# Attention groups 8 to 47: probabilities divided before they are split, and multiplied with V in column tiles

## What is computed

```python
# x, ctx: (16, 128, 1024); 32 heads in 8 groups; head width 32; K and V have 8 heads
query, key, value = layernorm(x) @ w_q.T, ctx @ w_k.T, ctx @ w_v.T
scores = einsum('bghnd,bgsd->bghns', query, key) / 32 ** 0.5
scores = where(mask, scores, finfo.min)
out    = einsum('bghns,bgsd->bghnd', softmax(scores), value)
x = x + out @ w_out.T
x1, x2 = split(layernorm(x) @ w12.T + b12)
x = x + (silu(x1) * x2) @ w3.T + b3
```

## Time and profile before

| | |
|---|---|
| median of 3 runs | 1041.44 us (1040.89 to 1043.1) |
| the profiled execution, first to last instruction | 1040.4 us |
| PE busy | 1017.7 us, 98% |
| DVE busy | 661.6 us, 64% |
| ACT busy | 447.3 us, 43% |
| POOL busy | 498.6 us, 48% |
| chain that ended last: PE's share | 87% |

### The profile page before, as it was taken

The page is one execution under the profiler, slowest core; times in us unless marked ns, Lnnn a source line. Parts: engine busy times, 40 slices in busy tenths (PEclk is TensorE's granted clock), DMA queues, the critical chain, the costliest instruction groups (busy, mean ns, idle before and its releaser), DMA issues.

```text
span 1040.4 us, 21876 instructions
## 1 busy us (share of the span) xinstructions
PE 1017.7 (98%) x8400; PEld 695.6 (67%) x8400; DVE 661.6 (64%) x2080; ACT 447.3 (43%) x983; POOL 498.6 (48%) x476
## 2 busy tenths in 40 slices
PE   7897999999999999999999999999999999999998
PEld 6786868869687696886655544444444888468853
DVE  6789977767787777888646234636864447625431
ACT  6768556557465574664766210123431112202100
POOL 2869923727337273379958596158742301212000
PEclk9999999999999999999999999999999999999999
DMA  9669686998989999789946715494758631974201
GB/s 367 227 160 197 168 216 168 222 247 222 248 211 229 230 245 244 179 236 232 268 94 123 253 71 203 94 345 160 272 200 185 235 112 40 236 230 122 83 31 51
DMA packets 230776, 199.12 MB, mean 191 GB/s; under 512 B 177040, under 2 KB 187280, under 8 KB 225808
## 3 DMA queue, kind: packets, MB, share of 16 engines
q1 hardware_dynamic: 230672, 197.72, 69.0%
HBM read 119.04 MB, written 35.65 MB: 149 GB/s over the span
## 4 chain that ended last, share of the span: by engine, by line
PE 87%; DVE 6%; DMA 1%; ACT 1%; issue 0%; SPq 0%; DVEq 0%
PE bank_dense L1349 52%; PE bank_spare L1349 13%; PE bank_score L1494 6%; PE bank_spare L1494 6%; PE bank_av L1494 3%; PE bank_score L1406 2%; DVE arena_attn L1820 2%; DVE arena_attn L1830 1%; PE bank_av L1424 1%; PE bank_av L1428 1%; PE bank_av L1426 1%; PE bank_dense L1366 1%; DMA k_scratch<-arena_in 1%; PE bank_spare L1358 0%; PE bank_dense L1358 0%
## 5 line engine op out<-in xcount | busy, mean ns | idle before, releaser
L1153 ACT ACTIVATE arena_attn<-arena_attn,arena_in 128x128 f32<-128x128 f32 x512 | 162.7, 391 | 94.6 <-DVE arena_in L1820 93.6
L1349 PE MATMUL bank_dense<-arena_rows,arena_in 128*128 128x256 f16 (+1 forms) x1272 | 175.2, 295 | 1.9 <-POOL arena_in L874 1.0
L936 POOL TENSOR_TENSOR arena_attn<-arena_attn 128x512 f16<-128x512 f32 x89 | 102.6, 1170 | 148.8 <-ACT arena_attn L1160 148.8
L1349 PE MATMUL bank_dense<-arena_attn,arena_rows 128*128 128x512 f16 x768 | 166.4, 379 | 0.0
L1349 PEld LDWEIGHTS bank_dense<-arena_rows,arena_in 128*128 128x128 f16 x1272 | 123.0, 98 | 43.1 <-DVE arena_in L1668 1.6
L1820 DVE CUSTOM_DVE_ANT_0 arena_attn<-bank_score,arena_in 128x128 f32<-128x128 f32 x512 | 143.5, 346 | 0.4 <-PE bank_score L1406 0.4
L1349 PEld LDWEIGHTS bank_dense<-arena_attn,arena_rows 128*128 128x128 f16 x768 | 75.2, 98 | 90.2
L1349 PE MATMUL bank_dense<-arena_out,arena_attn 128*128 128x512 f16 x576 | 127.8, 379 | 0.0
L1349 PEld LDWEIGHTS bank_dense<-arena_out,arena_attn 128*128 128x128 f16 x576 | 55.5, 98 | 63.3
L1349 PE MATMUL bank_spare<-arena_rows,arena_in 128*128 128x256 f16 (+1 forms) x648 | 87.6, 292 | 0.0
L1349 PE MATMUL bank_dense<-arena_out,arena_in 128*128 128x512 f16 x384 | 83.0, 379 | 0.0
(11 more groups left out here) (219 smaller groups left out, 1890.8 us busy)
## 6 DMA issues: line engine op xcount, KB each, us to landing
arena_rows<-x SPq DMA_DIRECT2D x32, 512.0 KB, 6.1
arena_in<-w_scratch SPq DMA_DIRECT2D x64, 256.0 KB, 3.1
arena_attn<-q_scratch SPq DMA_DIRECT2D x48, 256.0 KB, 4.5
arena_rows<-w_t SPq DMA_DIRECT2D x12, 1024.0 KB, 6.2
arena_rows<-ctx_t SPq DMA_DIRECT2D x8, 1024.0 KB, 6.1
q_scratch<-arena_attn SPq DMA_DIRECT2D x16, 512.0 KB, 5.1
x_scratch<-arena_rows SPq DMA_DIRECT2D x16, 512.0 KB, 3.8
arena_out<-x_scratch SPq DMA_DIRECT2D x16, 512.0 KB, 5.9
```

The source lines that it names most:

```text
L936: ins = pool.tensor_tensor(p_split[:, g % 2, u, 1], e[:, g % 2, u], p_split[:, g % 2, u, 0], ALU.subtract)
L1153: ins = act.activation(head, head, ACT.Exp, bias=neg_max[:, g % 2, h:h + 1], scale=-1.0)
L1349: ins = pe.matmul(dst, lhs(a, c), rhs(b, c), start=(c == chunks[0] and n == 0), stop=(c == chunks[-1] and n == 2))
```

## The change

For groups 8 to 47 (`NORMED`) the probabilities are divided by their sum before they are split into fp16 pairs, and the product with V is taken the other way round:

- **ACT** `exps`: each of the 8 exponentials also sums its output into `p_sum` (`accum_out`). `prob_hi(g)` no longer waits for the exponentials but for the division (`s_vnorm`, `s_pnorm`), and stands behind `scale_rows`.
- **DVE** `norm_prob(g, 0)` behind `attn_lo(g-3)` in step g, and `norm_prob(g, 1)` at the head of step g+1, ahead of `divide` and `mask_scores(g+1)`. Each is a reciprocal of 4 sums and a multiply of 512 columns of `e` in place, with the reciprocals broadcast. The reciprocals lie in SBUF for g = 8 and 9 and in `bank_av` (PSUM) from 10 on.
- **POOL** `norm_prob(g)`: where s is 3 or more it does the multiply of sequence 0; DVE then only scales the 4 reciprocals for it. In its order it stands behind `prob_lo(g-1)`.
- **PE** `weigh(g)`: V's 32 columns are the weights and the turned probabilities (128 columns) the moving operand; each of the four heads of a sequence has its own 32 columns of the array (`tile_position=(0, 32 j)`). 24 matmuls as before. The result is already turned; it goes to a bank of the rotation, in `turn_attn`'s place in step g+3, and `turn_attn(g)` and `divide(g)` are gone. The weigh at the end of step g+2 is gone too.
- `attn_hi`, `attn_lo` take the factor 2^-14 out again. Waits that meant "weigh(g) done" now look at `s_dense`; SP's `turn_prob(g)` waits for `weigh(g-2)`, which comes one step later than it did.

```diff
+NORMED = range(8, 48)
+P_SCALE = 2.0 ** 14
+def by_pool(g):
+    return g in NORMED and g % GROUPS >= 3
...
+        def weighed(g):
+            return (s_dense, done("a", g)) if g in NORMED else (s_av, divided_count(g))
...   (SP, turn_prob; PE and ACT wait in the same way)
                 if g >= 2:
-                    sp.wait_ge(s_av, g - 1)
+                    sp.wait_ge(*weighed(g - 2))
...   (POOL)
+            def norm_prob(g):
+                pool.wait_ge(s_vinv, normed_count(g, by_pool))
+                heads = e[:, g % 2, 0].rearrange("p (j n) -> p j n", j=HPG)
+                pool.tensor_tensor(heads, heads, inv.rearrange("p (j o) -> p j o", o=1).broadcast_to([P, HPG, SEQ]),
+                                   ALU.mult).then_inc(s_pnorm, 1)
...
-                    if GROUPS * (t - 1) + s > PLO_ALONE:
-                        prob_lo(GROUPS * (t - 1) + s - 1)
+                    g = GROUPS * (t - 1) + s
+                    if g > PLO_ALONE:
+                        prob_lo(g - 1)
+                    if by_pool(g):
+                        norm_prob(g)
...   (ACT)
-                    ins = act.activation(head, head, ACT.Exp, bias=neg_max[:, g % 2, h:h + 1], scale=-1.0)
+                    if g in NORMED:
+                        ins = act.activation(head, head, ACT.Exp, bias=neg_max[:, g % 2, h:h + 1], scale=-1.0,
+                                             accum_out=p_sum[:, g % 2, u, j:j + 1])
+                    else: ...
...
             def prob_hi(g):
-                act.wait_ge(s_exp, 2 * g + 2)
+                if g in NORMED:
+                    act.wait_ge(s_vnorm, vector_count(g, 1))
+                    if by_pool(g):
+                        act.wait_ge(s_pnorm, normed_count(g, by_pool))
+                else:
+                    act.wait_ge(s_exp, 2 * g + 2)
...   (PE, weigh)
+                if g in NORMED:
+                    dst = begin("a", g)
+                    terms_of_out = ((v_high, 0), (v_low, 0), (v_high, 1))
+                    for u in range(U):
+                        for n, (v, piece) in enumerate(terms_of_out):
+                            for j in range(HPG):
+                                ins = pe.matmul(dst[DH * j:DH * j + DH, SEQ * u:SEQ * u + SEQ],
+                                                v[:, a % 2, u, m, 0:DH], prob_t[:, g % 2, u, piece, j],
+                                                start=n == 0, stop=n == 2, tile_position=(0, DH * j))
+                    ins.then_inc(s_dense, 1)
+                    return
...
-                    if g >= 3:
+                    if g >= 3 and g - 3 in NORMED:
+                        weigh(g - 3)
+                    elif g >= 3:
                         turn_attn(g - 3)
...
-                    if g >= 2:
+                    if g >= 2 and g - 2 not in NORMED:
                         weigh(g - 2)
...   (DVE)
+            def norm_prob(g, u):
+                sums_inv = (inv_first if g < NORMED[2] else inv_bank)[:, g % 2, u]
+                dve.wait_ge(s_exp, 2 * g + u + 1)
+                dve.reciprocal(sums_inv, p_sum[:, g % 2, u]).then_inc(s_rec, 1)
+                dve.wait_ge(s_rec, half_count(g, u))
+                if u == 0 and by_pool(g):
+                    dve.tensor_scalar(inv, sums_inv, P_SCALE, None, ALU.mult).then_inc(s_vinv, 1)
+                    return
+                heads = e[:, g % 2, u].rearrange("p (j n) -> p j n", j=HPG)
+                dve.scalar_tensor_tensor(out=heads, in0=heads, scalar=P_SCALE,
+                                         in1=sums_inv.rearrange("p (j o) -> p j o", o=1).broadcast_to([P, HPG, SEQ]),
+                                         op0=ALU.mult, op1=ALU.mult).then_inc(s_vnorm, 1)
...   (DVE's program)
+                    if g - 1 in NORMED:
+                        norm_prob(g - 1, 1)
                     if g >= 3:
                         divide(g - 3)
                     mask_scores(g)
...
                     if g >= 3:
                         attn_lo(g - 3)
+                    if g in NORMED:
+                        norm_prob(g, 0)
```

More of the change, by code:

```diff
@@ L302, in later_unit, with normed_count, half_count, vector_count @@
     return UNITS * (f - PLAIN) + i
+def by_pool(g):
+    return g in NORMED and g % GROUPS >= 3
+def normed_count(g, kind=lambda n: n in NORMED):
+    return sum(kind(n) for n in range(g + 1))
+def half_count(g, u):
+    return U * normed_count(g - 1) + u + 1
+def vector_count(g, u):
+    return half_count(g, u) - normed_count(g, by_pool)
+def divided_count(g):
+    return g + 1 - normed_count(g)
 def plo_count(g):
@@ L409, in xattn_ffn @@
         kept, with_6, with_5, with_7 = [terms[:, 0], terms[:, 1]], terms[:, 2], terms[:, 3], terms[:, 4]
+        p_sum = part(arena_attn, 59, 1, F32)[:, 0:2 * U * HPG].rearrange("p (r u j) -> p r u j", r=2, u=U)
+        inv = part(arena_attn, 60, 1, F32)[:, 0:HPG]
+        inv_first = part(arena_attn, 61, 1, F32)[:, 0:2 * U * HPG].rearrange("p (r u j) -> p r u j", r=2, u=U)
         k_stack = part(arena_attn, 63, 4).rearrange("p (b g n) -> p b g n", b=2, g=4)
@@ L559, in xattn_ffn @@
         s_av, s_inv, s_avread = sem("av_done"), sem("inv_sum_done"), sem("attn_ready")
+        s_pnorm, s_vnorm = sem("prob_normed_by_pool"), sem("prob_normed_by_vector")
+        s_rec, s_vinv = sem("inv_sum_of_prob_done"), sem("inv_sum_for_pool_done")
         s_scales, s_cout = sem("block_scales_done"), sem("c_out_done")
@@ L810, in _ @@
             for k in range(2, 4):
-                sp.wait_ge(s_av, NG)
+                sp.wait_ge(*weighed(NG - 1))
                 sp.dma_start(w3_in[k], w3_t[k]).then_inc(s_w3load[k], 16)
@@ L1124, in attn_hi @@
                     act.wait_ge(s_dense, done("o", (g - RING) // GROUPS, 3))
-                act.activation(attn_t[:, g % RING, 0], bank("a", g)[:, 0:AB], ACT.Copy).then_inc(s_dhi, 1)
+                act.activation(attn_t[:, g % RING, 0], bank("a", g)[:, 0:AB], ACT.Copy,
+                               scale=1 / P_SCALE if g in NORMED else 1.0).then_inc(s_dhi, 1)
             def q_hi(t, m):
@@ L1141, in v_hi @@
                 if u == 0 and t >= 2:
-                    act.wait_ge(s_av, GROUPS * (t - 1))
+                    act.wait_ge(*weighed(GROUPS * (t - 1) - 1))
                 act.wait_ge(s_dense, done("v", t, u))
@@ L1152, in exps @@
                     head = e[:, g % 2, u, SEQ * j:SEQ * j + SEQ]
-                    ins = act.activation(head, head, ACT.Exp, bias=neg_max[:, g % 2, h:h + 1], scale=-1.0)
+                    if g in NORMED:
+                        ins = act.activation(head, head, ACT.Exp, bias=neg_max[:, g % 2, h:h + 1], scale=-1.0,
+                                             accum_out=p_sum[:, g % 2, u, j:j + 1])
+                    else:
+                        ins = act.activation(head, head, ACT.Exp, bias=neg_max[:, g % 2, h:h + 1], scale=-1.0)
                 ins.then_inc(s_exp, 1)
             def prob_hi(g):
-                act.wait_ge(s_exp, 2 * g + 2)
+                if g in NORMED:
+                    act.wait_ge(s_vnorm, vector_count(g, 1))
+                    if by_pool(g):
+                        act.wait_ge(s_pnorm, normed_count(g, by_pool))
+                else:
+                    act.wait_ge(s_exp, 2 * g + 2)
                 if g >= 2:
@@ L1269, in _ @@
                     unit_hi(second_unit(t, s))
-                    prob_hi(g)
                     if t < NB - 1 and s in (4, 6):
                         scale_rows(2 * t + s // 2)
+                    prob_hi(g)
                     if t == NB - 1 and s in (2, 6):
@@ L1362, in turn_attn @@
             def turn_attn(g):
-                pe.wait_ge(s_avread, g + 1)
+                pe.wait_ge(s_avread, divided_count(g))
                 dst = begin("a", g)
@@ L1416, in weigh @@
                     pe.wait_ge(s_dread, done("v", a, 1))
-                if g:
-                    pe.wait_ge(s_avread, g)
-                else:
+                if g == 0:
                     pe.wait_ge(*taken("ctx1"))
+                if divided_count(g - 1):
+                    pe.wait_ge(s_avread, divided_count(g - 1))
+                if g in NORMED:
[9 more added lines that the diff above has]
+                    return
                 for u in range(U):
@@ L1485, in seven_products @@
                         pe.wait_ge(s_exp, 2 * NG)
-                        pe.wait_ge(s_avread, NG)
+                        pe.wait_ge(s_avread, divided_count(NG - 1))
                     elif last % NP == 0:
@@ L1831, in prob_lo @@
                    .then_inc(s_plo, 1)
+            def norm_prob(g, u):
[10 more added lines that the diff above has]
+                                         op0=ALU.mult, op1=ALU.mult).then_inc(s_vnorm, 1)
             def divide(g):
+                if g in NORMED:
+                    return
                 av = B_AV[:, 0:VW * U * HPG].rearrange("p (h w) -> p h w", w=VW)
-                dve.wait_ge(s_av, g + 1)
```

(7 more changed lines are left out.)

1 line of the change is left out of this document (added).

## The result

| | before | after |
|---|---|---|
| median | 1042.09 us (4 runs, 1040.89 to 1043.1) | 1058.32 us (4 runs, 1055.67 to 1059.55) |
| profiled execution, first to last instruction | 1040.4 us | 1055.7 us |
| ratio | | 1.0156, 95% interval 1.0139 to 1.0173 |

The kernel became 16 us slower, where 6 were forecast. The time lies in the stated range (1035 to 1062), but the terms of the forecast don't hold: one is 13 us too high, another 17 us too low. Every ratio in this document compares executions that agree with each other; one of the ten of e7, at 1308.93 us, is left out of its ratio.

What follows compares the result with a forecast made beforehand. The prediction took PE's own stream as the bound, 98% busy. To the 1040.4 us span it added 3.0 for the weigh, 2.6 for the start and 1.0 for s = 7, 1047.0, giving a median of 1048 us, range 1035 to 1062.

Steps and rivals of the forecast that it cites:

- The new weigh: PE, groups 8 to 47: 0.90 us a group against 0.82 removed, +0.08 each, +3.0 us over 40 groups.
- The switch between tile shapes: PE entering and leaving small tiles among full matmuls: 0 to 0.25 us a weigh, taken at the full 0.25.
- The lower end: Least time for the new weigh's body on PE: 24 matmuls at the old rate of 0.025 us, 0.60.
- The second estimate: The new weigh's body from fp32 weight loads 0.11 us apart: 0.027 for 32 columns, 0.65 for 24.
- Rival B: PE's weigh: each set of tiles loads only after the set before finishes, 1.24 us a weigh, 1061 us; chance 0.10.
- Rival C: PE's weigh: the four column tiles run in turn, not side by side, +32 us, 1077 us; chance 0.07.
- Start-up: Steps 8 to 11: four norms ahead of divide(7) on DVE start step 11's scores late, +2.6 us once.
- The s = 7 steps: Norm ahead of the mask on DVE makes PE wait 0.2 us in each of five blocks, +1.0 us.
- the sentence on SP: SP's queue: only later loads stand behind turn_prob, and PE needs its data two steps on; priced at nothing.
- the loop of the short steps: Mask, exponentials and norm in short steps: about 6.1 us, under the step's 6.6, so priced at nothing.
- Rival D: DVE becomes the bound, with norms of 1.05 to 1.3 us instead of 0.82: 1054 us; chance 0.13.
- Rival A: PE's weigh: the switch between tile shapes is hidden, the whole weigh takes 0.60 us, 1036 us; chance 0.25.

Runs made afterwards that it cites:

- e7: The kernel of e1 without accumulators on ACT's exponentials, the sums left out: 1041.9 us, ratio 0.9978 to the kernel before.
- e8: The kernel of e1 with all 24 matmuls of a weigh on one column tile instead of four: 1073.84 us in one run.
- e2: The changed kernel without the division (no norms, POOL multiply or ACT accumulators), only the new weigh kept: 1034.37 us, ratio 0.991 to the kernel before.
- e11: The changed kernel itself, unaltered, measured again on another chip: 1059.18 us, ratio 1.0154 to the kernel before.
- e6: The kernel before with only SP's weight loads put ahead of turn_prob, as a control: 1044.25 us, ratio 1.001.
- e5: The kernel of e1 with the change applied from group 12 on instead of group 8: 1038.05 us, ratio 0.9949 to the kernel before.
- e1: The changed kernel with SP's three loads of the weights to be looked at put ahead of turn_prob: 1042.78 us, ratio 0.9988 to the kernel before.
- e3: The changed kernel with all norm multiplies on DVE and none on POOL: 1059.6 us, ratio 1.0154 to the kernel before.
- e12: The kernel of e1 with the weigh issued head by head, a head's three terms in a row: 1043.48 us in one run.
- e4: The kernel before with the load of the weights looked at in s = 6 issued only after that step's mask: 1063.95 us, ratio 1.019.

## Why the prediction was wrong

**The new weigh: too dear by 0.34 us a group.** Predicted 0.65 + 0.25; measured 0.34 + 0.2. The switch between tile shapes was priced right from the spread of step 44. The body was below both ends of its bound. The lower end took the rate of the old matmuls, 0.025, as a floor for any small matmul; but those loaded 128 columns of weights each, and four loads of 32 columns start within about 0.01 us. The second estimate divided the pitch of a pair of fp32 loads by four, and fp16 loads are not paced like that. Both "lower bounds" were prices of other work. The true floor was in the rows: four tiles side by side can't finish before the 0.057 of one, six sets make 0.34. Loads and matmuls of one weigh, timeline of after, show the overlap:

```profile
299.06 0.24 PE L1485 MATMUL bank_dense<-arena_attn,v_high 128*32 128x128 f16 x4
299.07 0.10 PEld L1485 LDWEIGHTS bank_dense<-arena_attn,v_low 128*32 128x32 f16 x4
299.13 0.23 PE L1485 MATMUL bank_dense<-arena_attn,v_low 128*32 128x128 f16 x4
299.13 0.16 PEld L1485 LDWEIGHTS bank_dense<-arena_attn,v_high 128*32 128x32 f16 x8
```

The second set's weights go in at 299.07 while the first set runs. Rival B, with its loads held back, would have needed 1.24 us a weigh; it is out. The rule behind it (the Trainium skill, page "TensorE: Matmul & The Clock Gate", section "The mechanism" in the part on tiling: a load overlaps matmuls in flight only on other rows) doesn't hold here. The Trainium skill's 2.38 for three tiles (same page, "Measured speedup vs the span model") is in the same direction as the 1.34 / 0.34 = 3.9 for four that e8 and after give. Rival C is out by e8, which is what C would have looked like. Summed over the groups, this term is -10 (e2), where +3 was forecast (40 x 0.08 is 3.2, and by the same terms rival B comes to 1062; neither changes anything).

**Start-up: right in mechanism and place.** Step 11's scores were to start 2.6 us late; they start 2.4 late against step 9's, by the wait for divide(6) and divide(7) on L1924 (2.2 and 1.4 us; 1.5 late in e11's profile, or 2.5 against e6's). Steps 11 and 12 lose another 0.9, where the shorter weigh should have given 0.5: out_proj waits for `o_low` (0.7) and `attn_lo` (0.5), which the sum left out. e5 confirms the cause by taking it away.

**The s = 7 steps: the step that failed.** +1.0 was forecast, +18.5 measured. The 0.2 us a block was a guess from the norm's length. e1 shows what DVE's own work costs there: 9.44 instead of 8.84, +0.6 a block, three times the guess. The rest, 15.6 us with the half clock in it, comes from the sentence on SP: "Queued behind it on SP are only later loads, and PE needs its data two steps on. Nothing." It priced the transposed probabilities' way and not that of the loads behind them. These had hardly any slack: in before DVE already waits 0.17 us for the one of s = 4, and the one of s = 6 lands at 295.61, where DVE takes it at 296.07. So the first is late for DVE as soon as `turn_prob` is, and its maximum then holds the next maximum and the next load. The prediction did see that `prob_hi` would come some 3 us later, and let POOL's idle time cover it; that time covers POOL, not the queue that waits for POOL.

**Covers that held.** ACT's accumulators (0.09 us each; e7), POOL's multiply (1.04 us; e3), the loop of the short steps (6.25 us a step, no wait in it), the later `turn_prob` for its own data (e1, e2). The norm on DVE measured 0.21 + 0.60 by starts, against the 0.82 of the prediction. Rival D is out: DVE is busy 74.35 of 90 us from 190 to 280 in after (67.98 in the earlier trace rows), and e1 takes the loss away without touching DVE.

**Rival A** had PE right and gave 1036; with the loads in order (e1) the same change gives 0.9988, and with the start-up gone (e5) 0.9949. That the forecast has the right sign and that the time lies in its range is luck: two errors, 13 us too high and 17.5 too low, partly cancel.

## What to carry to other kernels

When a change makes one transfer later, price each entry queued behind it by its own slack, from issue to first use; a load that lands 0.5 us before its reader has none, and what waits in that reader's queue multiplies it. A ring (load, reader, next load; or load, reader, norm, split, turn, next load) hands a lateness on from step to step: look for one before adding a wait to a chain. And a lower bound has to be the floor of the new work, not the price of the nearest old work.

## What the runs showed of the hardware that was not expected

- Four fp16 column tiles of 32 columns, with 128 moved columns each, run fully side by side: 24 matmuls take 0.34 us against 1.34 on one tile, in either order of issue (e8, e12). Going in and out among full matmuls costs 0.2 us.
- A short stand can cost more than itself. 0.6, 2.7 and 0.7 us of waiting in step 39 were followed by the granted clock at 0.50 and 5.11 us for a projection of 2.62. It doesn't come each time: with waits of 1.1, 2.0 and 0.3 in e4's step 31 the clock stayed at 1.00, and with 1.0, 2.0 and 0.3 in its step 39 it fell to 0.50.
- Of the norm's multiplies, those whose reciprocals lie in PSUM last the same each time, those of groups 8 and 9, with both operands in SBUF, do not (duration min/median/max in ns):

```profile
L1913 DVE SCALAR_TENSOR_TENSOR arena_attn<-arena_attn,bank_av x51: 686/687/689, 135.6 to 453.1; 128x512 f32<-128x512 f32 x51
L1913 DVE SCALAR_TENSOR_TENSOR arena_attn<-arena_attn x4: 691/738/1473, 118.7 to 130.2; 128x512 f32<-128x512 f32 x4
```

  These four are also the earliest, so place and time are not told apart, and what made one of them take 1.47 us was not tried. L1830's 2.11 in the earlier trace rows may be of the same kind.
